# The bottom features move into the spare rows of the pair strips: seven contraction chunks in the first layer instead of eight (a DLRM tower on one core)

## The chip, the core and the metric

The kernel runs on one core of a Trainium2 chip. Its time is the device time of one execution in microseconds (us). The core has five engines that run side by side and meet only at semaphores: TensorE (PE, with its weight loads shown as PEld), VectorE (DVE), ScalarE (ACT), GpSimd (POOL) and SyncE (SP). SP here only starts transfers; POOL starts the gathers and sets tiles to constants; 16 DMA engines move the data. TensorE writes to PSUM, and only DVE and ACT copy from there to SBUF.

## The reference

For each of 512 samples, 26 embedding rows of 128 numbers are looked up and put beside the sample's `bottom_output` row. All 351 dot products between pairs of the 27 vectors are formed. These and the bottom row itself (479 numbers) go through a tower of three layers.

```
e = stack([tbl_f[ids[:, f]] for f in range(26)], axis=1)         # 512 x 26 x 128
all_emb = concatenate([bottom[:, None, :], e], axis=1)           # 512 x 27 x 128
gram = einsum('bfd,bgd->bfg', all_emb, all_emb)
z = gram[:, TRIU_I, TRIU_J]                                      # 512 x 351
h = concatenate([z, bottom], axis=1)                             # 512 x 479
h = maximum(h @ W_top1 + b_top1, 0)                              # 479 -> 512
h = maximum(h @ W_top2 + b_top2, 0)                              # 512 -> 256
y = h @ W_top3                                                   # 256 -> 1
```

All is in float32.

## The kernel before

The samples go in four tiles of 128. Seven small tables (1,000 rows) are not gathered: in the opening each is multiplied with one-hot matrices for all 512 samples at once (`pick`, lines 413 and 422), and ACT puts the result into `static_t`, where slot 0 is the bottom feature, transposed. DVE makes the one-hot matrices (line 249) and the low halves of the tables (line 240). The other 19 tables are gathered by POOL, one indirect DMA per table and tile, 76 in all (line 214), into the single buffer `rows`. PE transposes the gathered rows in six turns per tile (`turn`, line 434), DVE and ACT copy them into `features` (line 223). A gather into a place of `rows` waits until the turn of the tile before has read it.

`products` (line 448) forms the dot products of four samples in one matmul, 32 matmuls per tile in four batches. `copy_pairs` (line 234) brings each batch from PSUM into `pairs`: 16 copies, 8 by DVE and 8 by ACT. `pairs` has 7 chunks of 128 rows; each chunk has four strips of 32 rows, of which 26 hold dot products. One row of the last chunk is set to 1.0 and carries the bias. The copies have 32 rows, except those of the last sample in each group of four, which have 26.

`layer1` (line 460) contracts over these 7 chunks and, as an eighth, over `static_t` slot 0 with the bottom features' weight rows. For each of four column groups `n` that is one matmul on the bottom features, issued ahead of the wait for the pair copies, and seven behind it. `layer2` (line 480) and `layer3` (line 487) follow. A float32 matmul stands in the trace as two records, so the 28 matmuls on `pairs` are 56 records.

The order is written out by hand. In the opening the queues follow the lists `OPENING_PE`, `OPENING_DVE`, `OPENING_ACT`. Tiles 1 to 3 are a hardware loop on each of PE, DVE and ACT; in one pass PE does turns 0 and 1 of tile t, then layer 1 of tile t-1, turns 2 and 3, half of layer 2, the rest of the turns, the other half, and the products of tile t. Layers 1 to 3 of the last tile stand behind the loop. POOL's program is straight: a few constants, among them the zeros of `pairs` (line 203) and the ones (line 205), a wait for `ids_all`, and the 76 gathers. SP's queue is straight too: ids, tables, the bottom rows (line 181), more ids and tables, then the weights (line 183).

Of the kernel before, what the change touches and what calls it, by code (L numbers as in the profile page):

```python
# [30 lines left out]
BGROUPS = 8  # L31
BATCHES = TILE // SPG // BGROUPS
# [14 lines left out]
EVEN, ODD = (NT + 1) // 2, NT // 2  # L47
LAST_ROWS = 96


# [3 lines left out]
OPENING_PE, OPENING_DVE, OPENING_ACT = [], [], []  # L54
for _i in range(PICKS):
    OPENING_PE.append(("pick", _i))
    OPENING_DVE.append(("pick", _i))
    OPENING_ACT.append(("high", _i))
    if _i == 0:
        OPENING_PE.append(("bottom", 0))  # L60
    if _i == 1:
        OPENING_DVE.append(("bottom", 0))
    if 1 <= _i < PICKS:
        OPENING_ACT.append(("out", _i - 1))

# [12 lines left out]

def dlrm_tower(nc, bottom, ids, picked_ids, picked, tables, w1, w2, b2, w3, out):
    f32, f32r, i32 = mybir.dt.float32, mybir.dt.float32r, mybir.dt.int32  # L80
    ALU, ACT = mybir.AluOpType, mybir.ActivationFunctionType

    with ExitStack() as ctx:  # L83
        def sb(name, shape, dt=f32):
            return ctx.enter_context(nc.sbuf_tensor(name, shape, dt))
# [4 lines left out]
        def sem(name):  # L90
            return ctx.enter_context(nc.semaphore(name))
# [11 lines left out]
        static_t = sb("static_t", [128, FIRST_G, BATCH])  # L103
        bottom_rows = sb("bottom_rows", [128, TILES, DIM])
        rows = sb("rows", [128, FEATURES - FIRST_G, DIM])
        features = sb("features", [128, TILE, SLOTS])
        pairs = sb("pairs", [128, CHUNKS, TILE])
        ident = sb("ident", [128, 128])
        w1_sb = sb("w1_sb", [128, CHUNKS + 1, HID1])
        w2_sb = sb("w2_sb", [128, HID1 // 128, HID2])  # L110
# [19 lines left out]
        bottom_in = sem("bottom_in")  # L130
        w1_in = sem("w1_in")
# [3 lines left out]
        ident_ready = sem("ident_ready")  # L135
# [11 lines left out]
        pads_ready = sem("pads_ready")  # L147
        last_pick_put = sem("last_pick_put")
        warm_ready = sem("warm_ready")
        bottom_turned = sem("bottom_turned")  # L150
        bottom_ready = sem("bottom_ready")
        turned = sem("turned")
# [4 lines left out]
        pairs_dve = sem("pairs_dve")  # L157
# [11 lines left out]
        @block.sync  # L169
        def _(sp):  # L170
            sp.dma_start(ids_all[:], ids).then_inc(ids_in, 16)
            sp.dma_start(table_raw[0][:, HALF:, :], picked[0][:, HALF:, :]).then_inc(first_half_in, 16)
            sp.dma_start(table_raw[0][:, 0:HALF, :], picked[0][:, 0:HALF, :]).then_inc(table_in[0], 16)
            for i in range(1, PICKS):
                sp.dma_start(ids_wide[:, i, :], picked_ids[i].partition_broadcast(128)).then_inc(wide_in[i], 16)
                if i >= 2:
                    sp.wait_ge(lo_ready, i - 1)
                    sp.wait_ge(hi_ready, i - 1)
                sp.dma_start(table_raw[i % 2][:], picked[i]).then_inc(table_in[i % 2], 16)
                if i == 1:  # L180
                    sp.dma_start(bottom_rows[:], bottom.rearrange("(t p) d -> p t d", p=TILE)).then_inc(bottom_in, 16)
            for c in range(CHUNKS + 1):
                sp.dma_start(w1_sb[:, c, :], w1[128 * c:128 * c + 128, :]).then_inc(w1_in, 16)
            sp.dma_start(w2_sb[:], w2.rearrange("(c p) n -> p c n", p=128)).then_inc(mlp_in, 16)
            sp.dma_start(b2_sb[:], b2).then_inc(mlp_in, 16)
            sp.dma_start(w3_sb[:], w3).then_inc(mlp_in, 16)
            sp.wait_ge(y_ready, 1 + TILES)
            sp.dma_start(out.rearrange("b n -> n b"), y_sb[:]).then_inc(out_done, 16)
            sp.wait_ge(out_done, 16)
# [34 lines left out]

        def copy_pairs(engine_copy, k, strips):

            view = pairs[:].rearrange("p q (k m s) -> p k s m q", k=BATCHES, s=SPG)
            for s in strips:
                for j in range(STRIPS):
                    n = strip_columns(j)  # L230
                    c = s * COLS + j
                    height = min(32, FIRSTS - 32 * s)
                    src = prod_ps[k % 2][32 * s:32 * s + height, :, c:c + STRIPS * (n - 1) + 1:STRIPS]
                    last = engine_copy(view[32 * j:32 * j + height, k, s, :, 0:n], src)  # L234
            return last

        @block.vector
        def _(dve):
# [29 lines left out]
            def pairs_out(t):  # L268
                for k in range(BATCHES):
                    dve.wait_ge(prods_done, BATCHES * t + k + 1)  # L270
                    copy_pairs(nc.vector.tensor_copy, k, (0, 1)).then_inc(pairs_dve, 1)

# [6 lines left out]
            for kind, n in OPENING_DVE:  # L279
                if kind == "pick":  # L280
                    pick_operands(n)
                elif kind == "turn":
                    features_out(0, n)
                else:
                    dve.wait_ge(bottom_turned, 1)
                    nc.vector.tensor_copy(static_t[:, 0, :], turn_ps[1][:].rearrange("p t b -> p (t b)")
                                          ).then_inc(bottom_ready, 1)
            dve.wait_ge(pads_ready, 2)
            dve.wait_ge(bottom_ready, 1)
            dve.wait_ge(picks_ready, PICKS - 1)  # L290
# [10 lines left out]
        def _(act):  # L301
# [32 lines left out]
            def pairs_out(t, first):  # L334
                for k in range(BATCHES):
                    act.wait_ge(prods_done, BATCHES * t + k + 1)
                    copy_pairs(nc.scalar.copy, k, (2, 3)).then_inc(pairs_act, 1)
                    if k == 0 and not first:
                        y_out(t - 1)
# [56 lines left out]
        def _(pe):  # L396
# [59 lines left out]
            def layer1_units(t, n, c, start, stop):  # L456
                k = LAST_ROWS if c == CHUNKS - 1 else 128
                rhs = static_t[:, 0, bass.ts(t, TILE)] if c == CHUNKS else pairs[0:k, c, :]

                return nc.tensor.matmul(mlp_ps[n // 2][:, n % 2, :], w1_sb[0:k, c, 128 * n:128 * n + 128], rhs,  # L460
                                        start=start, stop=stop, skip_group_check=True)

            def layer1(t, free):
                for n in (2, 3, 0, 1):
                    if n == 0:
                        pe.wait_ge(y_ready, free)
                    layer1_units(t, n, CHUNKS, n % 2 == 0, False)
                pe.wait_ge(pairs_dve, BATCHES * (t + 1))
                pe.wait_ge(pairs_act, BATCHES * (t + 1))
                for n in range(4):  # L470
                    for c in range(CHUNKS):
                        last = layer1_units(t, n, c, False, c == CHUNKS - 1)
                    if n % 2 == 1:
                        last.then_inc(h1_done, 1)
# [19 lines left out]
            for kind, n in OPENING_PE:  # L494
                if kind == "pick":
                    pick(n)
                elif kind == "bottom":
                    pe.wait_ge(ident_ready, 1)
                    pe.wait_ge(bottom_in, 16)
                    for t in range(TILES):  # L500
                        last = nc.tensor.transpose(turn_ps[1][:, t, :], bottom_rows[:, t, :], ident[:])
                    last.then_inc(bottom_turned, 1)
                else:
                    if n == 1:
                        pe.wait_ge(bottom_ready, 1)
                    turn(0, n)
            pe.wait_ge(pads_ready, 2)
            pe.wait_ge(last_pick_put, 1)
            products(0, True)
            pe.wait_ge(w1_in, 16 * (CHUNKS + 1))  # L510
            pe.wait_ge(mlp_in, 48)
# [65 lines left out]
```

## Time and profile before

| | |
|---|---|
| time, median of 3 runs | 136.47 us (135.78 to 136.93) |
| span of the profiled execution, first to last instruction | 134.1 us |
| PE, PEld busy | 114.4 us, 101.7 us |
| DVE, ACT busy | 71.7 us, 77.5 us |
| POOL busy | 83.8 us, all of it before 109.1 us |
| mean granted TensorE clock | 0.961 of full |

The time of the profiled execution is recorded as its span alone. The three runs lie 1.7 to 2.8 us above that span; the median lies 2.4 us above it.

Read the busy shares with care. They are averages over an opening (to about 47 us), three loop passes of about 21 us, and a tail. What an edit is worth depends on which wait ends last in its own stretch.

### The profile page before, as it was taken

How to read it: one execution, taken by the hardware profiler on the slowest of the kernel's cores; microseconds unless marked ns; L12 is line 12 of the kernel's file. 1: busy time of each engine (PE TensorE's matmuls, PEld its weight loads, DVE VectorE, ACT ScalarE, POOL GpSimd, SP SyncE). 2: the span in 40 equal slices, each digit the busy share in tenths (PEclk: the TensorE clock that was granted, in tenths of full speed). 3: DMA queues.
4: the chain of work that ended last, by engine and by line, in shares of the span. 5: the costliest groups of instructions: out<-in, count | busy, mean ns of one | idle time of the engine just before them, and what ended most of it. 6: DMA issues, size and time to landing. Idle time of an engine off the chain costs nothing.

```text
span 134.1 us, 2346 instructions
## 1 busy us (share of the span) xinstructions
PE 114.4 (85%) x804; PEld 101.7 (76%) x804; DVE 71.7 (53%) x198; ACT 77.5 (58%) x206; POOL 83.8 (62%) x86
## 2 busy tenths in 40 slices
PE   6599973999938897989999889999889739986993
PEld 6568853786727596989889889889879638985991
DVE  1499999149970039980428990408992310895000
ACT  4499990949861049941549961439981132995112
POOL 7488888778887777787777788777778740000000
PEclk9999996589997799999999999999999999999999
DMA  3997876458992121121221212112212120000000
GB/s 75 280 329 270 274 228 189 169 169 284 349 320 55 45 61 54 49 59 39 59 64 39 59 39 59 53 45 59 56 42 59 43 55 0 0 0 0 0 5 1
DMA packets 7241, 13.52 MB, mean 101 GB/s; under 512 B 2049, under 2 KB 3073, under 8 KB 7234
## 3 DMA queue, kind: packets, MB, share of 16 engines
q1 hardware_dynamic: 4658, 8.19, 18.7%
q0 software_dynamic: 2432, 4.99, 13.4%
q10 hardware_dynamic: 144, 0.26, 0.8%
q8 instruction: 4, 0.07, 0.2%
q14 instruction: 3, 0.02, 0.0%
HBM read 13.42 MB, written 0.00 MB: 100 GB/s over the span
## 4 chain that ended last, share of the span: by engine, by line
PE 34%; POOL 29%; issue 11%; DMA 10%; ACT 7%; DVE 5%; POOLq 1%; DVEq 0%; ACTq 0%
POOL rows L214 29%; PE mlp_ps L460 15%; PE prod_ps L448 10%; DMA rows<-in_tbl_dram,ids_all 7%; ACT pairs L234 6%; DVE pairs L234 5%; PE mlp_ps L480 3%; DMA ids_all<-in_ids_dram 3%; PE mlp_ps L413 2%; PE turn_ps L434 2%; PE mlp_ps L422 2%; PE mlp_ps L487 1%; POOLq L83 1%; ACT features L223 1%; ACT h L348 0%
## 5 line engine op out<-in xcount | busy, mean ns | idle before, releaser
L214 POOL DMA_INDIRECT rows<-in_tbl_dram,ids_all x76 | 81.4, 1070 | 24.4 <-issue 22.6
L234 DVE COPY pairs<-prod_ps 32x48 f32<-32x48 f32 (+1 forms) x128 | 31.7, 248 | 22.8 <-PE prod_ps L448 21.0
L234 ACT COPY pairs<-prod_ps 32x56 f32<-32x56 f32 (+3 forms) x128 | 31.9, 249 | 8.2 <-PE prod_ps L448 6.6
L448 PE MATMUL prod_ps<-features 128*122 128x104 f32 x256 | 30.3, 273 | 3.3 <-DVE pairs L234 1.3
L448 PEld LDWEIGHTS prod_ps<-features 128*122 128x122 f32 x256 | 28.4, 187 | 5.7 <-DVE pairs L234 2.9
L460 PE MATMUL mlp_ps<-pairs,w_sb 128*128 128x128 f32 (+1 forms) x224 | 26.0, 276 | 2.8 <-DVE pairs L234 1.8
L460 PEld LDWEIGHTS mlp_ps<-pairs,w_sb 128*128 128x128 f32 (+1 forms) x224 | 25.3, 192 | 3.5 <-DVE pairs L234 3.5
L223 DVE COPY features<-turn_ps 128x512 f32<-128x512 f32 (+1 forms) x12 | 10.0, 837 | 19.1 <-PE turn_ps L434 19.0
L434 PE MATMUL turn_ps<-ident,rows 128*128 128x128 f32 x76 | 12.2, 285 | 9.0 <-DMA rows<-in_tbl_dram,ids_all 8.6
L249 DVE TENSOR_SCALAR onehot<-ids_wide,row_of 128x512 fp32r<-128x512 int32 x42 | 17.3, 481 | 4.0 <-DMA ids_wide<-in_picked_ids_dram 4.0
L413 PE MATMUL mlp_ps<-onehot,table_hi 128*128 128x512 f32 x56 | 17.7, 462 | 1.5 <-ACT table_hi L313 1.5
L223 ACT COPY features<-turn_ps 128x512 f32<-128x512 f32 (+1 forms) x12 | 11.0, 915 | 11.3 <-PE turn_ps L434 11.3
L434 PEld LDWEIGHTS turn_ps<-ident,rows 128*128 128x128 f32 x76 | 8.9, 145 | 11.2 <-DMA rows<-in_tbl_dram,ids_all 7.3
L343 ACT ACTIVATE h<-mlp_ps 128x256 f32<-128x256 f32 x8 | 3.1, 384 | 21.9 <-PE mlp_ps L460 21.9
L422 PE MATMUL mlp_ps<-onehot,table_lo 128*128 128x512 f32 x56 | 15.4, 422 | 0.0
L413 PEld LDWEIGHTS mlp_ps<-onehot,table_hi 128*128 128x128 f32 x56 | 11.5, 217 | 4.7 <-ACT table_hi L313 1.7
L422 PEld LDWEIGHTS mlp_ps<-onehot,table_lo 128*128 128x128 f32 x56 | 11.9, 213 | 2.8
L309 ACT ACTIVATE distance<-ids_wide,minus_row 128x512 f32<-128x512 int32 x14 | 9.4, 716 | 2.5 <-DMA ids_wide<-in_picked_ids_dram 2.4
L240 DVE TENSOR_TENSOR table_lo<-table_raw,table_hi 128x1024 fp32r<-128x1024 f32 (+1 forms) x8 | 8.6, 1085 | 4.1 <-ACT table_hi L319 4.1
L480 PE MATMUL mlp_ps<-h,w_sb 128*128 128x128 f32 x64 | 8.6, 277 | 0.0
L322 ACT ACTIVATE onehot<-distance 128x512 fp32r<-128x512 f32 x14 | 8.0, 621 | 0.0
L480 PEld LDWEIGHTS mlp_ps<-h,w_sb 128*128 128x128 f32 x64 | 7.8, 192 | 0.2 <-ACT h L343 0.2
(31 smaller groups left out, 46.0 us busy)
## 6 DMA issues: line engine op xcount, KB each, us to landing
table_raw<-in_picked_dram SPq DMA_DIRECT2D x6, 512.0 KB, 3.6
w_sb<-in_W_top_dram SPq DMA_DIRECT2D x8, 256.0 KB, 5.2
ids_wide<-in_picked_ids_dram SPq DMA_DIRECT2D x6, 256.0 KB, 4.3
rows<-in_tbl_dram,ids_all POOLq DMA_INDIRECT x76, 2.5
table_raw<-in_picked_dram SPq DMA_DIRECT2D x2, 256.0 KB, 4.7
w_sb<-in_W_top_dram SPq DMA_DIRECT2D x1, 512.0 KB, 6.7
ids_wide<-in_picked_ids_dram ACTq DMA_DIRECT2D x1, 256.0 KB, 4.3
bottom_rows<-in_r_bottom_output_dram SPq DMA_DIRECT2D x1, 256.0 KB, 6.5
```

Of the source, the lines that this page charges most:

```text
L214: nc.gpsimd.indirect_dma_start(out=rows[:, slot - FIRST_G, :], out_offset=None, in_=tables[table], in_offset=bass.IndirectOffsetOnAxis(ap= ...
L223: return engine_copy(dst, turn_ps[g % 2][:, 0:len(turn), :])
L234: last = engine_copy(view[32 * j:32 * j + height, k, s, :, 0:n], src)
L240: return nc.vector.tensor_tensor(table_lo[i % 2][:, begin:end, :], table_raw[i % 2][:, begin:end, :], table_hi[i % 2][:, begin:end, :].bit ...
L249: nc.vector.tensor_scalar(onehot[i % 2][:, c, :], ids_wide[:, i, :], row_of[:, c:c + 1], None, ALU.is_equal).then_inc(onehot_ready, 1)
L309: nc.scalar.activation(distance[:, c, :], ids_wide[:, i, :], ACT.Abs, bias=minus_row[:, c:c + 1]).then_inc(distance_ready, 1)
L413: nc.tensor.matmul(acc, table_hi[i % 2][:, c, :], onehot[i % 2][:, c, :], start=(n == 0), stop=False)
L422: last = nc.tensor.matmul(acc, table_lo[i % 2][:, c, :], onehot[i % 2][:, c, :], start=False, stop=(n == RPP - 1))
L434: last = nc.tensor.transpose(turn_ps[g % 2][:, i, :], rows[:, slot - FIRST_G, :], ident[:])
L448: last = nc.tensor.matmul(prod_ps[k % 2][0:FIRSTS, m, 0:SPG * COLS], features[:, b:b + SPG, :].rearrange("p b f -> p (b f)")[:, 0:FIRSTS], ...
L460: return nc.tensor.matmul(mlp_ps[n // 2][:, n % 2, :], w1_sb[0:k, c, 128 * n:128 * n + 128], rhs, start=start, stop=stop, skip_group_check ...
L480: last = nc.tensor.matmul(mlp_ps[m][:, 2, :], w2_sb[:, c, 128 * m:128 * m + 128], h1[:, c, :], start=(c == 0), stop=(c == 3))
```

## The change

Each strip of 32 rows in `pairs` has 26 rows of dot products and one row (26) that is zero or, once, the ones. Rows 27 to 31 are spare: 5 rows in each of 26 strips, 130 in all. The change puts the 128 bottom features there, in the transposed form that the kernel's caller now lays out in memory, with their weight rows in the same places of `W_top1`. The first layer then contracts over seven chunks.

- `pairs` holds all 512 samples (7 x 512 numbers per partition instead of 7 x 128), since its spare rows are filled once for all tiles. POOL's two settings grow with it.
- SP fills the spare rows by four DMAs of 5 partitions each. They wait for `pads_ready` (POOL's settings) and stand ahead of the third table's ids.
- The bottom features come transposed from memory straight into `static_t` slot 0. Four transposes on PE, one copy on DVE and two semaphores go.
- All pair copies have 26 rows. In the loop their target and the right side of layer 1 depend on the tile number.
- Four matmuls per tile and one of eight weight DMAs (256 KB) go.

```diff
@@ opening lists
-    if _i == 0:
-        OPENING_PE.append(("bottom", 0))
-    if _i == 1:
-        OPENING_DVE.append(("bottom", 0))
@@
+FREE = SLOTS - FEATURES
+SPARE = [128 * q + 32 * j + FEATURES + i for j in range(STRIPS) for q in range(strip_columns(j)) for i in range(FREE)]
@@ tiles
-        bottom_rows = sb("bottom_rows", [128, TILES, DIM])
-        pairs = sb("pairs", [128, CHUNKS, TILE])
-        w1_sb = sb("w1_sb", [128, CHUNKS + 1, HID1])
+        pairs = sb("pairs", [128, CHUNKS, BATCH])
+        w1_sb = sb("w1_sb", [128, CHUNKS, HID1])
@@ sync
                 if i == 1:
-                    sp.dma_start(bottom_rows[:], bottom.rearrange("(t p) d -> p t d", p=TILE)).then_inc(bottom_in, 16)
-            for c in range(CHUNKS + 1):
+                    sp.dma_start(static_t[:, 0, :], bottom).then_inc(bottom_in, 16)
+                    sp.wait_ge(pads_ready, 2)
+                    for j in range(STRIPS):
+                        n = strip_columns(j)
+                        sp.dma_start(pairs[32 * j + FEATURES:32 * j + SLOTS, 0:n, :],
+                                     spare[FREE * j:FREE * j + FREE, 0:n, :]).then_inc(spare_in, 16)
+            for c in range(CHUNKS):
@@ copy_pairs
-            view = pairs[:].rearrange("p q (k m s) -> p k s m q", k=BATCHES, s=SPG)
+            view = pairs[:, :, bass.ts(t, TILE)].rearrange("p q (k m s) -> p k s m q", k=BATCHES, s=SPG)
-                    height = min(32, FIRSTS - 32 * s)
-                    src = prod_ps[k % 2][32 * s:32 * s + height, :, c:c + STRIPS * (n - 1) + 1:STRIPS]
-                    last = engine_copy(view[32 * j:32 * j + height, k, s, :, 0:n], src)
+                    src = prod_ps[k % 2][32 * s:32 * s + COLS, :, c:c + STRIPS * (n - 1) + 1:STRIPS]
+                    last = engine_copy(view[32 * j:32 * j + COLS, k, s, :, 0:n], src)
@@ vector
-                else:
-                    dve.wait_ge(bottom_turned, 1)
-                    nc.vector.tensor_copy(static_t[:, 0, :], turn_ps[1][:].rearrange("p t b -> p (t b)")
-                                          ).then_inc(bottom_ready, 1)
-            dve.wait_ge(bottom_ready, 1)
+            dve.wait_ge(bottom_in, 16)
@@ layer1
-                for n in (2, 3, 0, 1):
-                    if n == 0:
-                        pe.wait_ge(y_ready, free)
-                    layer1_units(t, n, CHUNKS, n % 2 == 0, False)
+                pe.wait_ge(y_ready, free)
                 pe.wait_ge(pairs_dve, BATCHES * (t + 1))
                 pe.wait_ge(pairs_act, BATCHES * (t + 1))
                 for n in range(4):
                     for c in range(CHUNKS):
-                        last = layer1_units(t, n, c, False, c == CHUNKS - 1)
+                        last = layer1_units(t, n, c, n % 2 == 0 and c == 0, c == CHUNKS - 1)
@@ tensor, opening
-                elif kind == "bottom":
-                    pe.wait_ge(ident_ready, 1)
-                    pe.wait_ge(bottom_in, 16)
-                    for t in range(TILES):
-                        last = nc.tensor.transpose(turn_ps[1][:, t, :], bottom_rows[:, t, :], ident[:])
-                    last.then_inc(bottom_turned, 1)
@@
-            pe.wait_ge(w1_in, 16 * (CHUNKS + 1))
+            pe.wait_ge(w1_in, 16 * CHUNKS)
+            pe.wait_ge(spare_in, 16 * STRIPS)
@@ weights in memory
-    w1[128 * CHUNKS:] = w[len(first):]
+    w1[SPARE[:DIM]] = w[len(first):]
```

POOL's program up to the first gather, before:

```order
L196 MEMSET ident 128x128
L198 AFFINE_SELECT ident<-ident 128x128 [waits ident_zero]
L201 MEMSET features 128x128x5
L203 MEMSET pairs 128x896
L205 MEMSET pairs 32x128 [waits pairs_zero]
L214 DMA rows<-in_tbl_dram,ids_all 128x128 [waits ids_in]
```

and changed:

```order
L199 MEMSET ident 128x128
L201 AFFINE_SELECT ident<-ident 128x128 [waits ident_zero]
L204 MEMSET features 128x128x5
L206 MEMSET pairs 128x3584
L208 MEMSET pairs 32x512 [waits pairs_zero]
L217 DMA rows<-in_tbl_dram,ids_all 128x128 [waits ids_in]
```

The order is the same; both settings of `pairs` are four times as long, and they stay ahead of the gathers.

PE's program behind the loop (last tile; `mlp_ps` holds the layers' sums, `pairs_act` and `pairs_dve` count the copied batches), before:

```order
L460 MATMUL mlp_ps<-static_t,w_sb 128x128 x2
L460 MATMUL mlp_ps<-static_t,w_sb 128x128 [waits y_ready]
L460 MATMUL mlp_ps<-static_t,w_sb 128x128
L460 MATMUL mlp_ps<-pairs,w_sb 128x128 [waits pairs_act,pairs_dve]
L460 MATMUL mlp_ps<-pairs,w_sb 128x128 x27
L480 MATMUL mlp_ps<-h,w_sb 128x128 [waits h1_ready]
```

and changed:

```order
L456 MATMUL mlp_ps<-pairs,w_sb 128x128 [waits pairs_act,pairs_dve,y_ready]
L456 MATMUL mlp_ps<-pairs,w_sb 128x128 x27
L474 MATMUL mlp_ps<-h,w_sb 128x128 [waits h1_ready]
```

The four matmuls that stood ahead of the wait for the pair copies are gone; the 28 behind it stay.

DVE's pair copies of one batch in the loop (`prods_done` counts PE's batches), before:

```order
L234 COPY pairs<-prod_ps 32x8x7 [waits prods_done]
L234 COPY pairs<-prod_ps 32x8x7
L234 COPY pairs<-prod_ps 32x8x6 x2
L234 COPY pairs<-prod_ps 32x8x7 x2
L234 COPY pairs<-prod_ps 32x8x6 x2
```

and changed (the first rows):

```order
L236 REGISTER_ALU [waits prods_done]
L236 COPY pairs<-prod_ps 26x8x7
L236 ISA
L236 COPY pairs<-prod_ps 26x8x7
L236 ISA
L236 COPY pairs<-prod_ps 26x8x6
L236 ISA
```

In the loop a register instruction, which works out the copy's target, now stands ahead of every copy; ACT's are alike.

## Rows read from the trace of the kernel before

**Rows 1.** Page, part 4: the chain that ended last, shares of the span.
```profile
PE 34%; POOL 29%; issue 11%; DMA 10%; ACT 7%; DVE 5%; POOLq 1%; DVEq 0%; ACTq 0%
```
**Rows 2.** Waits of POOL: engine, line, what waited for; us in total, times, longest.
```profile
POOL rows L214 <- issue: 22.6, 74, 0.3
POOL rows L214 <- DMA ids_all<-in_ids_dram: 1.6, 1, 1.6
POOL rows L214 <- PE turn_ps L434: 0.3, 1, 0.3
```
**Rows 3.** Timeline, opening: start, length, engine, line, operation, count, idle before and releaser.
```profile
0.92 0.20 POOL L196 MEMSET ident<- 128x128 f32 x1
2.18 0.84 POOL L203 MEMSET pairs<- 128x896 f32 x1
3.08 0.20 POOL L205 MEMSET pairs<- 32x128 f32 x1
3.71 0.95 SPq L175 DMA_DIRECT2D ids_wide<-in_picked_ids_dram  x1
4.86 1.10 POOL L214 DMA_INDIRECT rows<-in_tbl_dram,ids_all  x1 [1.58 <-DMA ids_all<-in_ids_dram]
5.15 2.62 DVE L249 TENSOR_SCALAR onehot<-ids_wide,row_of 128x512 fp32r<-128x512 int32 x6 [3.97 <-DMA ids_wide<-in_picked_ids_dram]
7.68 1.28 DVE L240 TENSOR_TENSOR table_lo<-table_raw,table_hi 128x512 fp32r<-128x512 f32 x2
7.79 2.09 POOL L214 DMA_INDIRECT rows<-in_tbl_dram,ids_all  x1 [0.30 <-issue]
12.46 1.34 ACT L309 ACTIVATE distance<-ids_wide,minus_row 128x512 f32<-128x512 int32 x2
```
**Rows 4.** Timeline, gathers beside DVE, and the last gather.
```profile
26.44 0.94 POOL L214 DMA_INDIRECT rows<-in_tbl_dram,ids_all  x1 [0.31 <-issue]
26.50 1.22 DVE L240 TENSOR_TENSOR table_lo<-table_raw,table_hi 128x1024 fp32r<-128x1024 f32 x1 [2.99 <-ACT table_hi L319]
108.14 0.94 POOL L214 DMA_INDIRECT rows<-in_tbl_dram,ids_all  x1 [0.30 <-issue]
```
**Rows 5.** Timeline of PE, opening.
```profile
22.16 1.09 PE L434 MATMUL turn_ps<-ident,rows 128*128 128x128 f32 x4 [2.91 <-DMA rows<-in_tbl_dram,ids_all]
40.60 0.44 PE L434 MATMUL turn_ps<-ident,rows 128*128 128x128 f32 x2 [2.38 <-DMA rows<-in_tbl_dram,ids_all]
```
**Rows 6.** Timeline of PE, last loop pass and tail.
```profile
99.24 6.49 PE L460 MATMUL mlp_ps<-pairs,w_sb 128*128 128x128 f32 x56 [0.54 <-ACT pairs L234]
106.94 0.66 PE L434 MATMUL turn_ps<-ident,rows 128*128 128x128 f32 x4 [0.77 <-DMA rows<-in_tbl_dram,ids_all]
110.69 0.44 PE L434 MATMUL turn_ps<-ident,rows 128*128 128x128 f32 x2 [2.09 <-DMA rows<-in_tbl_dram,ids_all]
120.47 1.08 PE L460 MATMUL mlp_ps<-static_t,w_sb 128*128 128x128 f32 x8
122.87 6.49 PE L460 MATMUL mlp_ps<-pairs,w_sb 128*128 128x128 f32 x56 [1.32 <-DVE pairs L234]
```
**Rows 7.** Stretches: us, busy of PE, PEld, DVE, ACT, POOL; clock, DMA share, GB/s.
```profile
21.30:28.10 6.80, 5.94 (x16) 4.88 (x17) 3.44 (x7) 4.16 (x6) 5.28 (x6) 0.50 0.51 170
41.80:45.10 3.30, 3.30 (x9) 2.58 (x8) 0.00 (x0) 0.00 (x0) 2.69 (x3) 0.50 0.24 62
45.20:120.00 74.80, 66.75 (x566) 62.59 (x565) 39.80 (x130) 43.10 (x144) 48.65 (x51) 1.00 0.17 45
```
**Rows 8.** Groups by line and shape: busy us, mean ns; and DVE's register instructions (ns).
```profile
L234 ACT COPY pairs<-prod_ps 26x56 f32<-26x56 f32 x32 | 8.3, 259 | 0.4
L234 ACT COPY pairs<-prod_ps 32x56 f32<-32x56 f32 x32 | 8.3, 258 | 7.1 <-PE prod_ps L448 6.6
L260 DVEq FUSED_REGOPS  x3: 46/46/46, 56.6 to 98.2; - x3
```

More of the change, by code:

```diff
@@ L76, in strip_columns, with dlrm_tower @@
     return sum(1 for q in range(CHUNKS) if 1 + STRIPS * q + j <= COLS)
-def dlrm_tower(nc, bottom, ids, picked_ids, picked, tables, w1, w2, b2, w3, out):
+SPARE = [128 * q + 32 * j + FEATURES + i for j in range(STRIPS) for q in range(strip_columns(j)) for i in range(FREE)]
+def dlrm_tower(nc, bottom, spare, ids, picked_ids, picked, tables, w1, w2, b2, w3, out):
     f32, f32r, i32 = mybir.dt.float32, mybir.dt.float32r, mybir.dt.int32
@@ L149, in dlrm_tower @@
         warm_ready = sem("warm_ready")
-        bottom_turned = sem("bottom_turned")
-        bottom_ready = sem("bottom_ready")
+        spare_in = sem("spare_in")
         turned = sem("turned")
@@ L223, in copy_features, with copy_pairs @@
             return engine_copy(dst, turn_ps[g % 2][:, 0:len(turn), :])
-        def copy_pairs(engine_copy, k, strips):
-            view = pairs[:].rearrange("p q (k m s) -> p k s m q", k=BATCHES, s=SPG)
+        def copy_pairs(engine_copy, t, k, strips):
+            view = pairs[:, :, bass.ts(t, TILE)].rearrange("p q (k m s) -> p k s m q", k=BATCHES, s=SPG)
             for s in strips:
@@ L270, in pairs_out @@
                     dve.wait_ge(prods_done, BATCHES * t + k + 1)
-                    copy_pairs(nc.vector.tensor_copy, k, (0, 1)).then_inc(pairs_dve, 1)
+                    copy_pairs(nc.vector.tensor_copy, t, k, (0, 1)).then_inc(pairs_dve, 1)
             nc.vector.memset(h1[:, 0, :], 0.0).then_inc(warm_ready, 1)
@@ L281, in _ @@
                     pick_operands(n)
-                elif kind == "turn":
+                else:
                     features_out(0, n)
-                else:
-                    dve.wait_ge(bottom_turned, 1)
-                    nc.vector.tensor_copy(static_t[:, 0, :], turn_ps[1][:].rearrange("p t b -> p (t b)")
-                                          ).then_inc(bottom_ready, 1)
             dve.wait_ge(pads_ready, 2)
-            dve.wait_ge(bottom_ready, 1)
+            dve.wait_ge(bottom_in, 16)
             dve.wait_ge(picks_ready, PICKS - 1)
@@ L336, in pairs_out @@
                     act.wait_ge(prods_done, BATCHES * t + k + 1)
-                    copy_pairs(nc.scalar.copy, k, (2, 3)).then_inc(pairs_act, 1)
+                    copy_pairs(nc.scalar.copy, t, k, (2, 3)).then_inc(pairs_act, 1)
                     if k == 0 and not first:
@@ L457, in layer1_units @@
                 k = LAST_ROWS if c == CHUNKS - 1 else 128
-                rhs = static_t[:, 0, bass.ts(t, TILE)] if c == CHUNKS else pairs[0:k, c, :]
-                return nc.tensor.matmul(mlp_ps[n // 2][:, n % 2, :], w1_sb[0:k, c, 128 * n:128 * n + 128], rhs,
+                return nc.tensor.matmul(mlp_ps[n // 2][:, n % 2, :], w1_sb[0:k, c, 128 * n:128 * n + 128],
+                                        pairs[0:k, c, bass.ts(t, TILE)],
                                         start=start, stop=stop, skip_group_check=True)
             def layer1(t, free):
-                for n in (2, 3, 0, 1):
-                    if n == 0:
-                        pe.wait_ge(y_ready, free)
-                    layer1_units(t, n, CHUNKS, n % 2 == 0, False)
+                pe.wait_ge(y_ready, free)
                 pe.wait_ge(pairs_dve, BATCHES * (t + 1))
@@ L496, in _ @@
                     pick(n)
-                elif kind == "bottom":
-                    pe.wait_ge(ident_ready, 1)
-                    pe.wait_ge(bottom_in, 16)
-                    for t in range(TILES):
-                        last = nc.tensor.transpose(turn_ps[1][:, t, :], bottom_rows[:, t, :], ident[:])
-                    last.then_inc(bottom_turned, 1)
-                else:
-                    if n == 1:
-                        pe.wait_ge(bottom_ready, 1)
+                else:
+                    if n == 0:
+                        pe.wait_ge(ident_ready, 1)
                     turn(0, n)
@@ L541 @@
     from concourse.bass_utils import run_bass_kernel_spmd as _run
-    arrays = {n: _np.ascontiguousarray(inputs[n]) for n in ["r_bottom_output", "W_top2"] + _GATHERED}
+    arrays = {n: _np.ascontiguousarray(inputs[n]) for n in ["W_top2"] + _GATHERED}
     for n in ("b_top2", "W_top3"):
@@ L547 @@
     arrays["picked_ids"] = _np.ascontiguousarray(ids[:, PICKED].T)
+    bottom = _np.ascontiguousarray(_np.asarray(inputs["r_bottom_output"]).T)
+    arrays["r_bottom_output"] = bottom
+    spare = _np.zeros((CHUNKS * 128, BATCH), _np.float32)
+    spare[SPARE[:DIM]] = bottom
+    arrays["spare"] = _np.ascontiguousarray(
+        spare.reshape(CHUNKS, STRIPS, SLOTS, BATCH)[:, :, FEATURES:].transpose(1, 2, 0, 3).reshape(-1, CHUNKS, BATCH))
     picked = _np.zeros((PICKS, 128 * RPP, DIM), _np.float32)
@@ L556 @@
     w = _np.asarray(inputs["W_top1"])
-    w1 = _np.zeros(((CHUNKS + 1) * 128, HID1), w.dtype)
+    w1 = _np.zeros((CHUNKS * 128, HID1), w.dtype)
     pair_row = _np.zeros((FEATURES, FEATURES), _np.int64)
@@ L571 @@
     out = nc.dram_tensor("out_0_dram", (BATCH, 1), _mybir.dt.float32, kind="ExternalOutput").ap()
-    dlrm_tower(nc, ap["r_bottom_output"], ap["ids"], ap["picked_ids"], ap["picked"],
+    dlrm_tower(nc, ap["r_bottom_output"], ap["spare"], ap["ids"], ap["picked_ids"], ap["picked"],
                {f: ap[f"tbl_{f}"] for f in GATHERED}, ap["W_top1"], ap["W_top2"],
```

## The prediction, before the changed kernel was run

> **What bounds the kernel now.** I read four views in this order. First the page's chain of waits [rows 1]. PE and POOL share it, and POOL has 29% and most of the "issue" beside it, although POOL computes nothing but gathers. Second, the waits of POOL [rows 2]. It waited once for data, 1.6 us for the ids at the start. The other 75 gaps are its own 0.30 us between gathers. The one put down to PE is 0.3 us long like the rest, so it was no wait. POOL therefore runs free: from its first gather at 4.86 us [rows 3] to the end of its 76th at 108.14 + 0.94 = 109.08 us [rows 4] it takes 104.2 us, whatever PE does. Third, the last pass of PE [rows 6]. PE waits for gathered rows 0.77 us at 106.94 and 2.09 us at 110.69. PE thus has 2.9 us to spare over POOL there, and the end is set by POOL's start, its stream, 1.6 us of landing, and 134.1 - 110.69 = 23.4 us of tail. Fourth, the tail itself: products, pair copies, layers. There layer 1 waits 1.32 us for the last pair copies [rows 6], after the four matmuls on the bottom features (8 records, 1.08 us) are done.
>
> So an edit counts if it moves POOL's first gather, POOL's stream, or the tail. In the opening and the loop PE can lose or gain almost 3 us unseen.
>
> **The removed matmuls, loop and tail: 0.** They stand ahead of a wait for pair copies that ends later than they do. In the tail it lasts 1.32 us more, in the pass at 99.24 us 0.54 us more [rows 6]. Without them PE waits longer and starts the other 28 at the same moment. Cover: the pair copies, which keep their length, since ACT's copies of 26 rows and of 32 rows take 259 and 258 ns [rows 8]. If that cover were gone the four would be worth 1.08 us in the tail.
>
> **The removed opening work (4 transposes, one DVE copy, one weight DMA of 256 KB): 0.** PE waits 2.91 us at 22.16 and 2.38 us at 40.60 for gathered rows [rows 5]. What it saves before them it waits. An earlier end of the weight stream can bring the rows awaited at 40.60 sooner, but that lands in PE's spare time too.
>
> **POOL's settings: +1.3 us, on the path.** The ident tile (128 numbers per partition) took 0.20 us and `pairs` (896) 0.84 us [rows 3]: (0.84 - 0.20) / 768 = 0.83 ns per number. For 3,584 numbers that gives 0.84 + 2,688 x 0.83 ns = 3.08 us, and for the ones (512 instead of 128) 0.20 + 0.32 = 0.52 us. The settings ended at 3.28 us and will end 2.24 + 0.32 = 2.56 us later, at 5.84. They were hidden behind the wait for the ids, which now has long ended. With the usual 0.30 us before a gather the first starts at 6.14 instead of 4.86: +1.3 us. Lower end: no gap, +1.0. Upper end: cost in proportion to size (3.36 and 0.80 us, end at 6.40), +1.8. I take 1.3, because the two rows show a fixed part. All later gathers shift alike.
>
> **What POOL meets at its new place: 0, between -1 and +1 us.** A gather normally takes 0.94 us. The one at 7.79 took 2.09, while DVE subtracted table halves from 7.68 to 8.96; the one at 26.44 kept its 0.94 although the same kind of DVE work ran from 26.50 [rows 3, 4]. So the meetings are a matter of tenths of a microsecond. In sum POOL was 81.4 us busy for 76 x 0.94 = 71.4, so 10 us are lost in this way, nearly all in the opening. A shift of 1.3 us deals these cards anew; one long meeting is about 1.1 us. The Trainium skill (SBUF — State Buffer, Who interferes with whom) says that VectorE in a two-port mode and GpSimd exclude each other for a whole instruction, while `tensor_tensor` holds up no descriptor generation. The 2.09 us gather beside a `tensor_tensor` speaks against the second half. By the first half the short setting of the ones, which now falls among the one-hot operations, would wait for one of them: the sum would be 139.3 instead of 138.9.
>
> **The clock in the tail: +1.1 us, between 0 and 3.4.** TensorE's granted clock stood at half (1.2 of 2.4 GHz) from 21.3 to 28.1 us and from 41.8 to 45.1 us [rows 7]. Each stretch came with an idle time of PE, 2.91 and 2.38 us [rows 5]. After 0.77, 2.09 and 1.32 us it stayed at full [rows 6, 7]. Four transposes took 1.09 us in the first stretch and 0.66 us at full clock [rows 5, 6]. Now the 1.08 us of matmuls between products and layer 1 go, and PE sits idle from about 120.5 to 122.87, 2.3 to 2.4 us: as long as the idle time that was followed by 3.3 us at half clock. Behind it stand 6.49 us of layer 1, in which PE is the bound. A stretch of 3.3 us at half clock loses half of it, 1.65 us. Not every execution need be caught, since 2.09 passed; two thirds of 1.65 is 1.1. Low end 0, high end 3.4 (half of the 6.8 us stretch). In the loop PE's idle time before layer 1 grows from 0.5 to 1.6 us, which no row shows to be followed by a lower clock, and 2.9 us of spare time are behind it.
>
> **Pair copies with a register instruction ahead of each: 0.** DVE and ACT do 32 copies each per tile, and the last tile's 32 are on the path. The nearest row is DVE's register instruction in the loop, 46 ns [rows 8]; it runs in the queue while the copy before, of some 250 ns, is still at work. Low end 0, high end 32 x 46 ns = 1.5 us. I take 0: the copy before it is five times as long.
>
> **SP's wait and the four spare DMAs: 0.** SP stands at `pads_ready` until about 5.8 us, then issues four transfers. Issues take up to 0.95 us [rows 3], so the third table's ids start at 7.6 to 9.6 instead of 3.71. All later tables queue behind them. ACT first reads these ids at 12.46 [rows 3]. If they are late, the third table is, and PE has its 2.91 us at 22.16, grown by POOL's 1.3, as cover. The spare rows themselves (0.27 MB) are needed by layer 1 of tile 0, after 56 us.
>
> **Sum.** 136.47 + 1.3 + 1.1 = **138.9 us**. The profiled span would go from 134.1 to 136.5; I put the same 2.4 us around it that the median shows before.
>
> **Rivals.**
> - *Delay alone* (0.28): the clock holds in the tail, as it did after 2.09 us. 136.47 + 1.3 = 137.8, with POOL's meetings 137.2 to 138.3.
> - *No change* (0.10): POOL starts 1.3 us later but has one long meeting with DVE less, since its first gathers now miss the first one-hot operations. 136.5.
> - *Faster* (0.06): the gathers that meet DVE's table subtractions slip past them. Each costs 1.1 us; with three fewer, 1.3 - 3.3 = -2.0, 134.5. It needs more than two to be a gain. For it: 10 us are lost there and the gather at 26.44 shows that one can slip past. Against: DVE's work hangs on the same arrivals and partly shifts with POOL.
> - *Copies slowed by the register instructions* (0.06): from the point at which a register instruction and a copy together outlast 0.26 us. Tail +1.5, so 140.4 with the clock. The two loop passes before would lose 3.0 us, about PE's spare time. For it: one stands ahead of each copy. Against: 46 ns.
> - *Late ids* (0.03): from the point at which the third table holds PE up beyond 2.91 + 1.3 us in the opening and 2.9 us at the end, about +1, 139.9. The Trainium skill (DMA: Bandwidth & Descriptors, Why a DMA increments its semaphore by 16 and not by 1) says that a transfer uses the largest number of engines up to 16 that divides its outer dimension, 5 for these; that would load five engines unevenly. No row of before shows such a transfer.
>
> **How the numbers follow.** My forecast has 0.47 (its own range 138.2 to 140.0). The range 136.9 to 140.5 takes in most of the delay alone, half of no change, and the slowed copies at their price. About 1% (1.4 us) is what a measurement here tells from no change: the border is 137.8. Slower: 0.47 + half of 0.28 + 0.09 = 0.70. Same: the other half and no change, 0.24. Faster: 0.06.
>
> **What would show it.** The setting of `pairs` at about 3.1 us and the first gather at 6.1 to 6.7; POOL again with no wait; PE idle for over 2 us before the last layer 1, with the same start after the last pair copy; a stretch at half clock within that layer 1, and its 56 records taking about 8 instead of 6.5 us; pair copies still 0.26 us from start to start. I am wrong if the gathers' stream is much shorter or longer than 104.2 us, if the clock holds (137.8), or if PE in the last pass no longer waits for gathered rows, for then the opening or the loop sets the end.

## The result and the profile after

| | before | changed |
|---|---|---|
| time, median of 4 runs | 136.7 us (135.78 to 137.07) | 139.91 us (138.46 to 140.43) |
| span of the profiled execution | 134.1 us | 138.4 us |
| mean granted TensorE clock | 0.961 | 0.938 |

The change made the kernel slower: the ratio is 1.0231, with a 95% interval of 1.0168 to 1.0293. I had forecast 138.9 us, in a range of 136.9 to 140.5. Every ratio here and below leaves out executions that are over 1.5% above their kernel's fastest, while every median takes them in.

The profiled execution of the changed kernel is the slowest of its four, whose spans are 136.3, 137.3, 138.1 and 138.4 us. That of the kernel before is probably the fastest of its four: the other recorded executions of that kernel lie 1.8 to 1.9 us above their spans, and its fastest time is 135.78 us. So the two traces lie 4.3 us apart, and the medians only 3.2.

The waits of POOL in the changed kernel (columns as in [rows 2]):

```profile
POOL rows L217 <- issue: 23.0, 76, 0.3
```

All 76 gaps are POOL's own now; the wait for the ids in [rows 2] is gone. The opening's timeline says where it went:

```profile
2.17 3.08 POOL L206 MEMSET pairs<- 128x3584 f32 x1
5.32 0.79 POOL L208 MEMSET pairs<- 32x512 f32 x1
6.13 1.32 SPq L183 DMA_DIRECT2D pairs<-in_spare_dram  x4
6.28 1.10 POOL L217 DMA_INDIRECT rows<-in_tbl_dram,ids_all  x1 [0.18 <-issue]
7.49 0.36 SPq L173 DMA_DIRECT2D ids_wide<-in_picked_ids_dram  x1
```

The large setting took 3.08 us, as worked out from [rows 3]. The small one took 0.79 instead of 0.52, and the gap before the first gather was 0.18 instead of the 0.30 that I had put. The first gather starts at 6.28 us and not at 4.86: +1.42 us.

The end of the loop and the tail, PE's timeline, against [rows 6]:

```profile
101.20 6.51 PE L456 MATMUL mlp_ps<-pairs,w_sb 128*128 x56 [1.53 <-DVE pairs L236]
111.94 0.54 PE L432 MATMUL turn_ps<-ident,rows 128*128 128x128 f32 x2 [2.19 <-DMA rows<-in_tbl_dram,ids_all]
125.55 8.12 PE L456 MATMUL mlp_ps<-pairs,w_sb 128*128 128x128 f32 x56 [2.27 <-DVE pairs L236]
133.50 2.24 PE L474 MATMUL mlp_ps<-h,w_sb 128*128 128x128 f32 x16
```

PE still waits for the last gathered rows, so POOL still sets when the tail begins: 111.94 instead of 110.69, +1.25 us. The tail then takes 138.4 - 111.94 = 26.5 us instead of 23.4. The four matmuls ahead of the last layer 1 are gone, PE idles 2.27 us there, and the 56 records that took 6.49 us [rows 6] take 8.12. The granted clock, by stretches (columns as in [rows 7]):

```profile
112.20:115.40 3.20, 3.20 (x18) 3.20 (x16) 0.00 (x0) 0.96 (x2) 0.00 (x0) 0.50 0.00 0
125.80:129.10 3.30, 3.30 (x18) 3.30 (x17) 0.00 (x0) 0.00 (x0) 0.00 (x0) 0.50 0.00 0
```

There are two stretches at half clock in the tail. The kernel before had none there: its row for the first of these stretches shows 28 records of PE where this one has 18.

```profile
112.20:115.40 3.20, 3.20 (x28) 2.82 (x29) 1.25 (x5) 1.50 (x6) 0.00 (x0) 1.00 0.00 0
```

The changed kernel also has a third new one, in the loop, again behind a wait for the last rows of a tile:

```profile
87.38 0.44 PE L432 MATMUL turn_ps<-ident,rows 128*128 128x128 f32 x2 [2.10 <-DMA rows<-in_tbl_dram,ids_all]
88.30:91.60 3.30, 3.30 (x17) 3.22 (x16) 0.00 (x0) 0.53 (x2) 2.40 (x3) 0.50 0.18 50
```

It costs nothing in the end, since PE waits 2.19 us for POOL's rows in the pass behind it. In the opening the changed kernel has one stretch less, that of 3.3 us in [rows 7]. So the mean clock alone does not give the time: one execution of the changed kernel had 0.937 and a span of 136.3 us, another 0.938 and 138.4.

For this pair of traces the account closes. The last turn comes 1.25 us later. From it to the first pair copy it takes 116.72 - 111.94 = 4.78 us instead of 114.08 - 110.69 = 3.39: +1.39, the first stretch. From that copy to layer 1 it takes 8.83 instead of 8.79: +0.04. From layer 1 to layer 2, 7.95 instead of 6.33: +1.62, the second stretch. The rest is 4.9 us in both. Together 4.3 us, the difference of the spans. Between the medians less of it is the clock's. Outside of the span a changed execution takes 2.0 to 2.2 us and one of the kernel before 1.8 to 1.9, about 0.3 us more, for a reason that no run shows. With 1.25 us for POOL, 3.2 - 1.25 - 0.3 leaves about 1.6 us for the clock in a typical execution (an estimate).

### The profile page after: what moved, and what is told of

It reads as the page before. It is cut to its first block, busy times and chain, and to the rows that moved or that the text cites. A ratio compares the mean times of both kernels' runs of the same rounds, so it can differ in the third digit from the quotient of the medians.

```text
span 138.4 us, 2485 instructions
## 1 busy us (share of the span) xinstructions
PE 114.6 (83%) x768; PEld 101.6 (73%) x768; DVE 71.7 (52%) x197; ACT 77.2 (56%) x206; POOL 86.3 (62%) x86
## 4 chain that ended last, share of the span: by engine, by line
POOL 61%; issue 19%; PE 12%; ACT 2%; DMA 2%; POOLq 1%; DVE 1%; DVEq 0%; ACTq 0%
POOL rows L217 57%; PE mlp_ps L456 6%; PE prod_ps L446 3%; PE mlp_ps L474 3%; POOL pairs L206 2%; DMA rows<-in_tbl_dram,ids_all 2%; ACT pairs L236 2%; POOLq L83 1%; DVE pairs L236 1%; POOL pairs L208 1%; POOL features L204 0%; PE turn_ps L432 0%; ACT y_sb L351 0%; ACTq L236 0%; PE mlp_ps L481 0%
## 5 line engine op out<-in xcount | busy, mean ns | idle before, releaser
L236 DVE COPY pairs<-prod_ps 26x56 f32 (+3 forms) x128 | 31.4, 245 | 23.8 <-PE prod_ps L446 22.1
L236 ACT COPY pairs<-prod_ps 26x56 f32 (+3 forms) x128 | 31.7, 247 | 10.3 <-PE prod_ps L446 8.4
L446 PE MATMUL prod_ps<-features 128*122 128x104 f32 x256 | 32.7, 284 | 3.0 <-ACT pairs L236 2.0
L446 PEld LDWEIGHTS prod_ps<-features 128*122 128x122 f32 x256 | 30.7, 199 | 5.4 <-DVE pairs L236 3.0
L456 PE MATMUL mlp_ps<-pairs,w_sb 128*128 (+3 forms) x224 | 27.7, 287 | 6.8 <-DVE pairs L236 5.3
L456 PEld LDWEIGHTS mlp_ps<-pairs,w_sb 128*128 128x128 f32 (+1 forms) x224 | 26.9, 202 | 7.7 <-issue 7.7
L432 PEld LDWEIGHTS turn_ps<-ident,rows 128*128 128x128 f32 x76 | 8.9, 143 | 10.7 <-issue 5.1
L420 PE MATMUL mlp_ps<-onehot,table_lo 128*128 128x512 f32 x56 | 14.7, 406 | 0.0
L420 PEld LDWEIGHTS mlp_ps<-onehot,table_lo 128*128 128x128 f32 x56 | 11.2, 201 | 2.5
L474 PE MATMUL mlp_ps<-h,w_sb 128*128 128x128 f32 x64 | 9.7, 301 | 0.0
L474 PEld LDWEIGHTS mlp_ps<-h,w_sb 128*128 128x128 f32 x64 | 8.8, 213 | 0.2 <-ACT h L341 0.2
```

Source lines behind the costliest of these rows:

```text
L236: last = engine_copy(view[32 * j:32 * j + COLS, k, s, :, 0:n], src)
L420: last = nc.tensor.matmul(acc, table_lo[i % 2][:, c, :], onehot[i % 2][:, c, :], start=False, stop=(n == RPP - 1))
L432: last = nc.tensor.transpose(turn_ps[g % 2][:, i, :], rows[:, slot - FIRST_G, :], ident[:])
L446: last = nc.tensor.matmul(prod_ps[k % 2][0:FIRSTS, m, 0:SPG * COLS], features[:, b:b + SPG, :].rearrange("p b f -> p (b f)")[:, 0:FIRSTS], ...
L474: last = nc.tensor.matmul(mlp_ps[m][:, 2, :], w2_sb[:, c, 128 * m:128 * m + 128], h1[:, c, :], start=(c == 0), stop=(c == 3))
```

## The experiments

Two things limit what they say. The chips that ran e1 to e7 took 169 to 180 us for the kernel before too. On them DVE, ACT and PE stand still for several us at a time in the loop, and POOL waits for PE's turns. The kernel before has these standstills as well, so they are not the change's; their cause stayed open. There the total time says little, and I read only the opening and the tail, which have no such standstill. e8 to e11 ran on a chip where the kernel before took 137.35 us. For them I give all six executions, since one more stretch at half clock is just what is looked for.

**e1, e6: VectorE sets `pairs`** (the same kernel twice).

```diff
 POOL
-            nc.gpsimd.memset(pairs[:], 0.0).then_inc(pairs_zero, 1)
-            nc.gpsimd.memset(pairs[64:96, CHUNKS - 1, :], 1.0).then_inc(pads_ready, 1)
 VectorE, before the opening list
+            nc.vector.memset(pairs[:], 0.0).then_inc(pairs_zero, 1)
+            nc.vector.memset(pairs[64:96, CHUNKS - 1, :], 1.0).then_inc(pads_ready, 1)
```

> The changed kernel with one thing taken back: VectorE, which is idle then, sets pairs to zeros and ones, and GpSimd goes from its pads to the gathers. Theory (GpSimd's start sets the end, plus a half clock where TensorE idles): first gather at 4.9 us again, last rows 1.3 to 1.4 us earlier, median 139.9 - 1.4 = 138.5, ratio to before about 1.013; TensorE still idles over 2 us before the last layer 1. Rival (the late ids and the opening make the loss): the first gather moves, but the time stays at 139.9, ratio 1.023. A third (copies slowed by register instructions): also 139.9.

> The changed kernel with pairs set by VectorE, once more, for the same reason. Theory: the first gather is back at 4.8 us and the last rows with it, and what is left of the loss is the half clock in the last layer 1 (56 records in 8.1 instead of 6.5 us) and sometimes ahead of the last products: ratio about 1.010 to 1.015 instead of 1.023. Rival (late ids and register instructions): 1.023 as the changed kernel.

Opening of e1:

```profile
1.86 3.04 DVE L277 MEMSET pairs<- 128x3584 f32 x1 [0.69 <-issue]
4.75 1.10 POOL L214 DMA_INDIRECT rows<-in_tbl_dram,ids_all  x1 [2.50 <-DMA ids_all<-in_ids_dram]
```

The setting is as long on DVE, but lies where DVE had nothing to do, and the first gather is back at 4.75 us (e6: 5.00), again right behind the ids. The last layer 1 is not mended: 8.12 us after 2.28 us of idle time (e6: 7.95). The place of the delay is shown; its worth in the total is not. The ratios, 1.0187 (1.0022 to 1.0353) and 1.0019 (0.9912 to 1.0125), come from two series of the same kernel. The second excludes the 1.023 of the rival and reaches the 1.010 of the theory, but where POOL waits 15 us and more for PE I count it for neither.

**e3, e5: the kernel before with the wide `pairs` tile alone** (the same kernel twice).

```diff
-        pairs = sb("pairs", [128, CHUNKS, TILE])
+        pairs_wide = sb("pairs", [128, CHUNKS, BATCH])
+        pairs = pairs_wide[:, :, 0:TILE]
```

> The kernel before with the wide pairs tile alone: GpSimd sets all 7 x 512 numbers per partition, the work uses the first 128 columns as before. All else, the eighth chunk included, is as before. Theory: the setting takes 3.1 us, the first gather starts at 6.1 to 6.3, and the time is 136.6 + 1.3 to 1.4 = 138.0, ratio 1.010, with the clock full in the tail. Rival (GpSimd's delay is taken up by idle time later): ratio 1.000.

> The kernel before with the wide pairs tile alone, once more: on the last chip the queues of VectorE and ScalarE stood still for several us at a time in every kernel, the one before included, so that the sum of the loop said nothing. Theory: where they do not, the first gather at 6.0 instead of 4.9 us costs 1.1 to 1.4 us, ratio 1.008 to 1.010. Rival (taken up later): 1.000.

Opening of e5:

```profile
5.32 0.52 POOL L206 MEMSET pairs<- 32x512 f32 x1
6.01 1.10 POOL L215 DMA_INDIRECT rows<-in_tbl_dram,ids_all  x1 [0.18 <-issue]
```

The tile's width alone moves the first gather to 6.01 us; the large setting took 3.08 us here too. The small setting took 0.52 us, as worked out; 0.79 and 0.75 us in the changed kernel and e2. The ratios are 1.0105 (0.9889 to 1.0322) and 0.9928 (0.9814 to 1.0041): inconclusive, since POOL waits over 20 us for PE on these chips and its start cannot set the end.

**e2: four filling matmuls ahead of the last layer 1** of the changed kernel.

```diff
+            for _ in range(4):
+                nc.tensor.matmul(turn_ps[0][:, 0, :], ident[:], ident[:], start=True, stop=True)
             layer1(TILES - 1, TILES)
```

> The changed kernel with four idle-time matmuls (8 records, about 1.1 us, on the unit matrix into a free PSUM tile) in front of the last layer 1, where the bottom features' matmuls stood in the kernel before. Theory (the idle time costs the clock): TensorE's idle time there falls from 2.3 to about 1.2 us, the 56 records of the last layer 1 take 6.5 us in place of 8.1, median 139.9 - 1.1 to 1.6 = 138.3 to 138.8, though they compute nothing. Rival (the clock is no cost, or falls by chance): no change, 139.9.

```profile
156.68 1.08 PE L518 MATMUL turn_ps<-ident 128*128 128x128 f32 x8
159.12 6.49 PE L456 MATMUL mlp_ps<-pairs,w_sb 128*128 128x128 f32 x56 [1.37 <-DVE pairs L236]
```

Work that computes nothing, in the place of the removed work, brings the idle time down to 1.37 us and layer 1 back to 6.49 us. The ratio, 1.0176 (1.0120 to 1.0232), carries the standstills.

**e4: the kernel before without the four matmuls.**

```diff
-                for n in (2, 3, 0, 1):
-                    if n == 0:
-                        pe.wait_ge(y_ready, free)
-                    layer1_units(t, n, CHUNKS, n % 2 == 0, False)
+                pe.wait_ge(y_ready, free)
```

> The kernel before without the four matmuls per tile on the bottom features; the bottom features' part of the first layer is left out of the result, and nothing else is moved. Theory: TensorE does 16 matmuls less and gains nothing, since it waits for the pair copies; in the tail it idles over 2 us and loses up to 1.6 us at half clock in most executions, median 136.6 + 0.5 to 1.6, ratio 1.004 to 1.012. Rival (work removed from the busiest engine counts): 16 x 0.27 us less at most, 4 of them (1.1 us) in the tail, ratio 0.992 or lower.

```profile
162.87 8.12 PE L460 MATMUL mlp_ps<-pairs,w_sb 128*128 128x128 f32 x56 [2.24 <-DVE pairs L234]
```

The mirror of e2: without the cover layer 1 takes 8.12 us, in a kernel that is otherwise the one before. The ratio, 1.0429 (1.0321 to 1.0537), has the sign, not the size, of the theory.

**e7: both taken back**, e1's and e2's edits together in the changed kernel.

> The changed kernel with both suspected costs taken back at once: VectorE sets pairs (so GpSimd's first gather is at 4.8 us), and four matmuls on the unit matrix fill TensorE's idle time ahead of the last layer 1. The late ids and the register instructions stay. Theory: nearly all of the loss goes; where the engines are not held up otherwise, ratio to before 1.000 to 1.006 (the half clock ahead of the last products may stay in some executions), last layer 1 in 6.5 us. Rival (late ids, register instructions): 1.015 to 1.023 stays.

The last layer 1 took 6.49 us after 1.37 us of idle time. For the total the run is inconclusive: 172.2 us against 174.59, and no ratio is on record for it.

**e8 to e11: no gathers in tiles 1 to 3.**

```diff
-            for t in range(TILES):
+            for t in range(1):
                 for g, turn in enumerate(TURNS):
@@
-                pe.wait_ge(rows_in[g], 16 * len(TURNS[g]) * (t + 1))
+                pe.wait_ge(rows_in[g], 16 * len(TURNS[g]))
```

Tiles 1 to 3 then work on tile 0's gathered rows, and POOL's stream no longer paces the loop. e8 is the kernel before with this edit, e9 adds e4's, e10 is the changed kernel with it, e11 adds e2's to e10. On this chip the kernel before had no standstills either, so e8 can't say whether they hang on the gathers.

> A base for the next three: the kernel before with the gathers of tile 0 alone; tiles 1 to 3 work on tile 0's gathered rows, so the result of these tiles is not the reference's. It takes GpSimd and its stream off the path and leaves TensorE's program as it is. Theory: TensorE no longer waits for rows in the last pass (2.9 us less), span about 131, time about 133.6. If the standstills of VectorE and ScalarE on the later chips have to do with the gathers, they are gone here; if not, it takes over 160 us.

> The same (tile 0's gathers alone), and the four matmuls per tile on the bottom features are left out too, with their part of the result. Against e8: theory (idle time costs the clock, the matmuls were free): last layer 1 in 8.1 instead of 6.5 us, time +1.6, or more if the loop's idle times also cost the clock. Rival (TensorE's work counts): -1.1 us in the tail and up to -1.1 in each loop pass.

> The changed kernel with tile 0's gathers alone, tiles 1 to 3 on tile 0's gathered rows. Theory: GpSimd's 1.3 us later start matters only for the rows of tile 0, so against e9 within 1.5 us; last layer 1 in 8.1 us. Rival (the register instructions slow the pair copies): each of the loop's copy phases longer by 1.5 us or more, so against e9 +4.5 us.

> As e10, with four matmuls on the unit matrix ahead of the last layer 1. Theory: 1.6 us less than e10, the last layer 1 in 6.5 us. Rival: no change.

| | median of 6 (us) | spans of the six (us) | last layer 1 in the profile |
|---|---|---|---|
| e8 | 133.23 | 128.8 to 133.4 | 6.49 |
| e9 | 133.73 | 128.9 to 134.9 | 6.49 |
| e10 | 133.17 | 128.7, 129.1, 130.9, 131.1, 131.7, 131.8 | 7.96 |
| e11 | 131.77 | 128.5, 128.7, 129.1, 129.4, 129.5, 129.6 | 6.49 |

First, the removed matmuls were free, as long as the clock held. The spans of e8 vary by some 4 us, and the two profiled openings differ by as much, so I compare the two profiles from the first products on, where the clock is full in both: 133.2 - 48.80 = 84.4 us with the 16 matmuls, 128.9 - 44.53 = 84.4 without.

```profile
117.65 6.49 PE L460 MATMUL mlp_ps<-pairs,w_sb 128*128 128x128 f32 x56 [2.35 <-ACT pairs L234]
```

This row of e9 is the one case in which over 2.2 us of idle time before the last layer 1 were followed by a full clock. Its 6.49 us, and a median only 0.5 us above e8's, are a miss of e9's expectation of 8.1 us and +1.6.

Second, the filler keeps the last layer 1 at 6.49 us: e11's median is 131.77 us against e10's 133.17. e10's spans fall into two groups, two at 129 with a mean clock of 0.973 and 0.974, and four at 131 to 132 with 0.961, which is one stretch of 3.3 us at half clock more; e11's all lie with the first. The profiled execution of e10 is of the second group, and its row places that stretch in the last layer 1; for the other three the place is not shown:

```profile
118.42 7.96 PE L456 MATMUL mlp_ps<-pairs,w_sb 128*128 128x128 f32 x56 [2.27 <-DVE pairs L236]
```

e11's row shows 6.49 us after 1.37 us of idle time. The gain of 1.4 us stands in the medians of all six alone. By the ratios to the kernel before, 0.9656 (0.9602 to 0.9711) for e11 and 0.9608 (0.951 to 0.9706) for e10, the filler is no gain. What it does to the clock is shown by the traces; its worth in the time is not shown beyond doubt.

Third, the register instructions cost nearly nothing. From one layer 1 to the next e8 takes 101.12 - 80.26 = 20.86 us, and e10 97.51 - 76.51 = 21.00:

```profile
80.26 6.49 PE L460 MATMUL mlp_ps<-pairs,w_sb 128*128 128x128 f32 x56 [0.56 <-ACT pairs L234]
101.12 6.49 PE L460 MATMUL mlp_ps<-pairs,w_sb 128*128 128x128 f32 x56 [0.58 <-ACT pairs L234]
```

```profile
76.51 6.51 PE L456 MATMUL mlp_ps<-pairs,w_sb 128*128 x56 [1.52 <-DVE pairs L236]
97.51 6.51 PE L456 MATMUL mlp_ps<-pairs,w_sb 128*128 x56 [1.53 <-DVE pairs L236]
```

That is 0.14 us per pass, where the rival asked for 1.5. e9, which has e10's matmuls without the register instructions, takes 96.78 - 75.90 = 20.88. The same rows show the loop without gathers: PE's idle time grew from 0.6 to 1.5 us, layer 1 started no sooner, and the clock held.

All traces together, for the last layer 1: behind 1.32 to 1.39 us of idle time (the kernel before, e2, e3, e5, e7, e8, e11) it took 6.49 us seven times out of seven. Behind 2.24 to 2.35 us (the changed kernel, e1, e4, e6, e9, e10) it took 7.95 to 8.12 us five times out of six.

## Why the prediction was right, and where its size was off

**Removed matmuls, 0: right.** As work they were worth nothing: PE waited 2.27 us in the tail and 1.53 us at 101.20 where it had waited 1.32 and 0.54 [rows 6]. e8 and e9 are equal from the first products on.

**POOL's settings, +1.3 us: right.** The large setting was to take 3.08 us and took 3.08. The first gather came 1.42 us later, for the small setting took 0.27 us more than worked out and the gap 0.12 less. The last rows came 1.25 us later. e1 and e3 move the first gather with the setting alone, in both directions. That the delay reaches the end rests on the two traces of before and after, where POOL never waits and PE waits for POOL's last rows in both. No experiment showed it in the total.

**What POOL meets, 0: right within its range, and by luck so near.** From the first gather to the last turn it took 111.94 - 6.28 = 105.7 us instead of 105.8, but the meetings were others: the longest gathers took 2.92 and 2.39 us, at 36.96 and 40.18, against 2.32 at 15.21 before. The gather at 12.00 in the changed kernel took 1.64 us, and DVE did nothing in that time but a table subtraction (11.60 to 12.82). This agrees with the prediction that a `tensor_tensor` does hold up a gather, against the Trainium skill (SBUF — State Buffer, Who interferes with whom), which takes descriptor generation to be free of it. By the same section's exclusion of VectorE in a two-port mode and GpSimd, the prediction gave 0.4 us more for the small setting. The traces show 0.27 us more in the changed kernel, 0.23 in e2 and nothing in e3 and e5, though DVE was at its one-hot operations each time; no run shows what decides between these.

**The clock in the tail, +1.1 us: right in mechanism for the last layer 1, too small in sum.** The stretch there cost 1.62 us (1.65 worked out). Five of six traces with such an idle time have it, and four of e10's six executions may by their spans. That this is near the two thirds of the forecast is partly luck: the share rested on one wait of 2.09 us that had passed. What I did not price is the second stretch, ahead of the last products, +1.39 us. I had counted PE's wait of 2.09 us for the last rows [rows 6] as one after which the clock stays. In the changed kernel the same wait is 2.19 us, and the clock fell; in the pass before it fell after 2.10 us. So the step that was mis-sized is the clock's: 3.0 us in the profiled execution, about 1.6 in a typical one, not 1.1. The median lies 1.0 us above the forecast: about 0.5 of that is the clock's, 0.3 lies outside of the span, and 0.2 is the kernel before itself, whose median moved from 136.47 to 136.7. Whether the second stretch has to do with the change is open: the wait is there in both kernels. Two of eleven executions of the kernel before on the chip of e8 to e11 had a mean clock of 0.950 and 0.951 and spans of 137.9 and 138.8 us, against 133.3 to 137.0 for the other nine. So extra time at half clock meets that kernel now and then too, but no trace shows where.

**Register instructions, 0: right**, 0.14 us per pass. DVE's take 57 ns and ACT's 46, beside copies of about 245 ns:

```profile
L236 DVEq FUSED_REGOPS  x93: 57/57/71, 67.8 to 124.2; - x93
```

**SP's wait and the spare DMAs, 0: right for the end, too mild for the opening.** The third table's ids were issued at 7.49 us and ACT could read them at 18.16, not at 12.46 [rows 3]. PE's first turn waited for rows until 19.84, where the kernel before had them by 14.98 without a wait:

```profile
18.16 1.34 ACT L307 ACTIVATE distance<-ids_wide,minus_row 128x512 f32<-128x512 int32 x2 [5.14 <-DMA ids_wide<-in_picked_ids_dram]
19.84 0.97 PE L432 MATMUL turn_ps<-ident,rows 128*128 128x128 f32 x4 [4.37 <-DMA rows<-in_tbl_dram,ids_all]
```

The ids were 10.7 us under way, where the median before was 4.3. The rival's condition came true, for the third table started at 21.56 us after 4.37 + 0.75 us of idle time of PE. Its price did not: the first products start at 45.10 us, and at 47.19 in the kernel before. The cover held, since PE waits for gathered rows anyway.

Where this came from can be seen in the traces' record of the single packets. The four spare transfers move as 20 packets of 12 and 14 KB, one for each partition, and some of them are under way from 7.79 to 16.49 us. From 8 to 16 us the gathers' packets took 0.55 us on average, and 0.17 in the kernel before. From 4 to 8 us, before them, the packets of 2 KB took 0.10 us, as in the kernel before (0.11), and from 16 us on the gathers' packets were back at 0.19. So it is in every trace: 0.48 to 0.61 us in the seven kernels that have the spare transfers, 0.17 to 0.18 in the six that have not, and the first turn starts at 19.3 to 20.8 us in the former and at 15.0 to 16.2 in the latter. Not only the ids came late, as the rival has it, but the gathered rows too, and not for POOL's later start, which e1, e6 and e7 do not have and e3 and e5 do. No run takes the spare transfers alone out of the changed kernel, though; its bottom features also come by another load. The rule of the Trainium skill (DMA: Bandwidth & Descriptors, Why a DMA increments its semaphore by 16 and not by 1) would put each of these transfers on 5 engines; no run shows which engine a packet was on.

## What to carry to other kernels

Work that stands ahead of a wait is free as long as it ends before the wait does, and can be worth more than nothing: here it kept PE busy, and without it the matmuls behind the wait ran slower in five of six traces. Ask of every shortcut on TensorE what fills its place. And a setting that is hidden behind one load has only that load's time to grow: 1.3 us were left, and the tile was made four times as wide on the engine whose stream of gathers sets the end, while VectorE was idle. And a small load can go with slow others: beside 0.27 MB in 20 long packets the gathers' packets took three times as long, and only PE's spare time in the opening hid it.

## What was not expected of the hardware

The fall of the clock after an idle time is not a matter of its length alone: it stayed after 2.35 us (e9) and 2.09 us (before), and fell after 2.10 and 2.19 us (changed kernel) and 2.24 us (e4). An idle time of 1.4 us or less never brought it down in the tail.

The version that these results point to was not run: the settings on VectorE, the four filling matmuls, and half of layer 2 ahead of the last turn, to fill the wait for the last rows with real work. Whether it is faster than the kernel before is open.
